# Cross-attention added to 32 batches on one core: four rows per partition and attention by halves of 64 queries

## The reference

```python
q = (tgt @ Wq.T).reshape(B, N, NH, dk).transpose(0, 2, 1, 3)
k = (memory @ Wk.T)...; v = (memory @ Wv.T)...
probs = softmax(einsum('bhqd,bhkd->bhqk', q, k) / sqrt(dk))
att = einsum('bhqk,bhkd->bhqd', probs, v).transpose(0, 2, 1, 3).reshape(B, N, D)
return tgt + att[0]
```

## Time and profile before

| | us |
|---|---|
| median of 3 runs | 190.15 (189.57 to 190.52) |
| profiled execution | 188.74 |
| its span | 186.6 |
| TensorE busy | 127.9 |
| DVE / ACT / POOL busy | 105.7 / 96.3 / 80.7 |

### The profile page before, as it was taken

One profiled execution on the slowest core, in us unless ns is written; L12 is line 12 of the kernel. 1 busy time (PEld: TensorE's weight loads), 2 busy tenths in 40 slices (PEclk: granted clock), 3 DMA queues, 4 the chain that ended last, 5 costly groups with the idle time before them and its releaser, 6 DMA issues.

```text
span 186.6 us, 3382 instructions
## 1 busy us (share of the span) xinstructions
PE 127.9 (69%) x1240; PEld 94.0 (50%) x1240; DVE 105.7 (57%) x171; ACT 96.3 (52%) x225; POOL 80.7 (43%) x45
## 2 busy tenths in 40 slices
PE   6999999999995978998889998798881000000000
PEld 6878877668663756775657666565550000000000
DVE  0455646643709999636699766945618999300000
ACT  2525535566476789679698778898860000000000
POOL 1000000000009999800099996399966999200000
PEclk9999999999999999999999999999999555555555
DMA  6999999999998999999999999999999999999996
GB/s 211 378 359 418 410 409 410 408 407 407 383 410 293 331 332 344 343 305 382 395 386 398 386 367 404 403 407 404 406 416 416 408 422 421 412 418 421 421 421 258
DMA packets 31968, 71.52 MB, mean 383 GB/s; under 512 B 1872, under 2 KB 10064, under 8 KB 31824
## 3 DMA queue, kind: packets, MB, share of 16 engines
q1 hardware_dynamic: 31952, 71.31, 99.9%
HBM read 37.75 MB, written 33.55 MB: 382 GB/s over the span
## 4 chain that ended last, share of the span: by engine, by line
PE 52%; DVE 14%; ACT 13%; issue 6%; DVEq 1%; POOL 0%; ACTq 0%; POOLq 0%
PE bank L387 12%; PE bank L367 8%; ACT probs L586 7%; PE bank L322 6%; PE bank L356 6%; PE bank L345 6%; DVE slots L719 5%; ACT probs_t L594 5%; PE bank L314 5%; PE bank L398 4%; DVE slots L709 3%; DVE neg_max L666 3%; PE bank L469 3%; DVE slots L702 1%; PE bank L409 1%
## 5 line engine op out<-in xcount | busy, mean ns | idle before, releaser
L272 POOL TENSOR_TENSOR slots<-slots,att_rows 128x512 f32<-128x512 f32 (+1 forms) x27 | 43.4, 1650 | 70.0 <-DVE att_rows L691 70.0
L586 ACT ACTIVATE probs<-bank,neg_max 128x512 f32<-128x512 f32 x64 | 44.9, 702 | 12.1 <-DVE neg_max L666 11.7
L666 DVE TENSOR_REDUCE neg_max<-bank 128x1 f32<-128x512 f32 x64 | 41.8, 682 | 11.9 <-PE bank L367 11.8
L387 PE MATMUL bank<-ident,probs 128*128 128x128 f32 x256 | 39.8, 281 | 7.8 <-ACT probs L586 6.7
L594 ACT COPY probs_t<-bank 128x512 f32<-128x512 f32 x64 | 37.7, 592 | 10.8 <-PE bank L387 10.0
L387 PEld LDWEIGHTS bank<-ident,probs 128*128 128x128 f32 x256 | 28.1, 140 | 21.3 <-ACT probs L586 17.1
L367 PE MATMUL bank<-k_t,x_q 32*128 32x512 f32 x192 | 24.1, 425 | 0.0
L278 POOL TENSOR_TENSOR slots<-slots,att_rows 128x1024 f32<-128x1024 f32 x8 | 18.6, 2377 | 4.8 <-DVE att_rows L691 4.8
L286 POOL TENSOR_TENSOR slots<-slots,att_rows 128x2048 f32<-128x2048 f32 x4 | 18.0, 4532 | 3.4 <-DVE att_rows L691 3.4
L702 DVE TENSOR_TENSOR slots<-slots,bank 128x512 f32<-128x512 f32 (+1 forms) x21 | 17.7, 856 | 0.1
L398 PE MATMUL bank<-probs_t,v 128*32 128x128 f32 x512 | 17.3, 276 | 0.7 <-ACT probs_t L594 0.7
(11 more groups left out here) (41 smaller groups left out, 98.6 us busy)
## 6 DMA issues: line engine op xcount, KB each, us to landing
slots<-in_x_dram SPq DMA_DIRECT2D x19, 1024.0 KB, 14.5
slots<-in_x_dram SPq DMA_DIRECT2D x26, 512.0 KB, 8.6
out_dram<-slots SPq DMA_DIRECT2D x13, 1024.0 KB, 14.1
out_dram<-slots SPq DMA_DIRECT2D x22, 512.0 KB, 8.7
out_dram<-slots SPq DMA_DIRECT2D x32, 256.0 KB, 3.6
ctx_raw<-in_ctx_dram SPq DMA_DIRECT2D x1, 1024.0 KB, 4.9
wq_raw<-in_L_xattn_Wq_dram SPq DMA_DIRECT2D x1, 1024.0 KB, 9.1
wv_raw<-in_L_xattn_Wv_dram SPq DMA_DIRECT2D x1, 1024.0 KB, 11.8
```

The source lines that it names most:

```text
L272: nc.gpsimd.tensor_tensor(xs, xs, a.unsqueeze(1).to_broadcast([P, BPS, a.shape[1]]), ALU.add).then_inc(added[g], 1)
L387: last = nc.tensor.transpose(bank[:, PT_BANK + h % 2, t * P:(t + 1) * P], probs[:, h % 2, t * P:(t + 1) * P], ident[:, :])
L586: nc.scalar.activation(probs[:, h % 2, :], bank[:, h % S_BANKS, :], ACT.Exp, bias=neg_max[:, h:h + 1], scale=1.0, accum_out=row_sum[:, h:h ...
L666: nc.vector.tensor_reduce(neg_max[:, h:h + 1], bank[:, h % S_BANKS, :], AX_X, ALU.max, negate=True).then_inc(max_ready, 1)
```

## The change

- A slot holds four adjacent rows per partition of four batches: partition (p, b) holds rows 4p to 4p + 3 of a tile of 128 rows, in 8 KB of memory in one piece. There are 8 groups per row tile and 18 slots. Stores of tiles 0 and 1 are halves of a slot (two rows, 4 KB pieces, 512 KB), those of tiles 2 and 3 whole slots (1 MB).
- Attention goes by halves H of 64 queries (two per tile) with all heads. A unit stacks two heads: partitions 0 to 63 are one head's 64 queries, 64 to 127 another's. Each half has 8 units.
- q and k are kept in fp32 as they are; scores are one full-fp32 matmul per head in a tile of 32 rows and 64 columns, in place of three fp32r passes. k_t needs no low part, and DVE evacuates q_t.
- x of batch 0 is turned by `turn_x0`, 16 matmuls with x as the stationary operand and every fourth column of the identity moving.
- `lay_out_sums` brings row sums to the transposed layout by matmuls, DVE inverts them there, and `normalize` scales the transposed attention while it copies each value four times side by side, for the four batches. `turn_left` and `turn_right` turn it back, the left 256 columns into a PSUM bank for DVE, the right 256 by way of ACT's `copy_right` to SBUF for POOL. DVE adds every left side, POOL every right side; each store waits for both.
- `sum_group` takes the place of `weigh_values`, with 64 moving columns; all four groups of a half share one region of a bank.

The core of the diff follows (within a part, lines that are only removed are mostly left out):

```diff
-BPS = 2
-ROWS = 2
+BATCHES = 4
+ROWS = 4
+HALF = ROWS // 2
...
-    GROUPS = B // BPS
-    SLOTS = GROUPS + 1
-    PAIR = 2
-    PAIRS = HEADS // PAIR
+    GROUPS = B // BATCHES
+    SLOTS = 2 * GROUPS + 2
+    QP = P // ROWS
+    QH = P // 2
+    SIDE = D // 2
+    HALVES = 2 * T
+    UNITS = HEADS // 2
+    PAIRS = UNITS // 2
     S_BANKS = 4
     PT_BANK, BACK_BANK, ATT_T_BANK = 4, 6, 7
-    PT_SLOTS = 6
+    PT_SLOTS = 5
...
+    x_rows = x.rearrange("b (j p r) d -> j p b (r d)", p=QP, r=ROWS)
...
+            def store_half(H, g):
+                sp.wait_ge(left_added, added_through(H, g))
+                sp.wait_ge(right_added, added_through(H, g))
+                sp.dma_start(out_rows[H // 2, :, g * BATCHES:(g + 1) * BATCHES,
+                                      H % 2 * HALF * D:(H % 2 + 1) * HALF * D],
+                             by_batch(slot(H // 2, g, half_rows(H)))).then_inc(stored[H // 2][g], 16)
...
             LAG = 3
             for g in range(GROUPS):
+                store_half(0, g)
             for g in range(GROUPS):
+                store_half(1, g)
                 if g >= LAG:
+                    reload_first(g - LAG)
+            for g in range(GROUPS - LAG, GROUPS):
+                reload_first(g)
             for g in range(GROUPS):
+                store_half(2, g)
+            for g in range(GROUPS):
+                store_half(3, g)
+                if g >= LAG:
+                    reload_second(g - LAG)
+            for g in range(GROUPS - LAG, GROUPS - 2):
+                reload_second(g)
+            for j in range(2, T):
+                for g in range(GROUPS):
+                    store(j, g)
...
+            for H in range(HALVES):
+                out_of_turn_bank(pool, H, RIGHT_SIDE)
+                for g in range(GROUPS):
+                    pool.wait_ge(loaded[H // 2][g], 16)
+                    xs = side_of(H, g, RIGHT)
+                    nc.gpsimd.tensor_tensor(xs, xs, att_right[:, H % 2, :, :], ALU.add).then_inc(right_added, 1)
...
+            def turn_x0(j):
+
+                pe.wait_ge(loaded[j][0], 16)
+                bank_free("x0_t", j)
+                ps = job_bank("x0_t", j)
+                for c in range(C):
+                    for r in range(ROWS):
+                        at = c * P + r * QP
+                        last = mm(ps[:, at:at + QP], slot(j, 0)[:, r, c * P:(c + 1) * P], first_batch,
+                                  start=True, stop=True)
+                last.then_inc(bank_filled, 1)
...
+            def scores(H, m, units):
+
+                queries = slice(H % 2 * QH, (H % 2 + 1) * QH)
+                for s in range(2):
+                    for i in units:
+                        g, rows = 2 * m + s, slice(i * DK, (i + 1) * DK)
+                        last = mm(bank[s * QH:(s + 1) * QH, i, :], q_t[rows, H // 2 % 2, g, queries], k_t[rows, g, :],
+                                  start=True, stop=True, tile_position=(i * DK, s * QH))
...
+            def lay_out_sums(H, m):
+
+                pe.wait_ge(exp_ready, H * UNITS + (m + 1) * HPG)
+                if H > 0:
+                    pe.wait_ge(att_t_ready, sums_through(H, 2 * m) - 1)
+                for s in range(2):
+                    for i in range(HPG):
+                        u = m * HPG + i
+                        last = mm(laid_sums(H, m)[i * DK:(i + 1) * DK, s, :],
+                                  row_sum[:, H % 2, u:u + 1].to_broadcast([P, DK]), ident[:, s * QH:(s + 1) * QH],
+                                  start=True, stop=True, tile_position=(0, i * DK))
+                last.then_inc(sums_laid, 1)
+
+            def sum_group(H, g):
+                m, queries = g // 2, slice(g % 2 * QH, (g % 2 + 1) * QH)
+                out_of_turn_bank(pe, H, m * HPG + HPG - 1)
+                pe.wait_ge(inverse_ready, inverses_through(H, m))
+                if sums_through(H, g) > 1:
+                    pe.wait_ge(att_t_ready, sums_through(H, g) - 1)
                 for t in range(T):
                     for i in range(HPG):
                         h = g * HPG + i
-                        last = mm(att_t_ps[i * DK:(i + 1) * DK, g, :], v[:, t, h * DK:(h + 1) * DK],
-                                  probs_t[:, (j * HEADS + h) % PT_SLOTS, t, :], start=(t == 0), stop=(t == T - 1),
+                        last = mm(bank[i * DK:(i + 1) * DK, ATT_T_BANK, 0:QH], v[:, t, h * DK:(h + 1) * DK],
+                                  probs_t_of(H, m * HPG + i)[:, t, queries], start=(t == 0), stop=(t == T - 1),
                                   tile_position=(0, i * DK))
                 last.then_inc(att_t_summed, 1)
...
+            def turn_rows(ps):
+
+                for r in range(HALF):
+                    for g in range(2):
+                        at = (r * 2 + g) * P
+                        queries = att_t[:, g, r * QP:(r + 1) * QP, :].rearrange("p q b -> p (q b)")
+                        last = nc.tensor.transpose(ps[:, at:at + P], queries, ident[:, :])
+                return last
+
+            def turn_left(H):
+
+                pe.wait_ge(att_t_ready, sums_through(H, 1))
+                if H > 0:
+                    pe.wait_ge(left_added, added_through(H - 1, GROUPS - 1))
+                turn_rows(bank[:, BACK_BANK, :]).then_inc(back_ready, 1)
+
+            def turn_right(H):
+
+                pe.wait_ge(att_t_ready, sums_through(H, HG - 1))
+                turn_bank_free(H, RIGHT_SIDE)
+                turn_rows(turn_bank(H, RIGHT_SIDE)).then_inc(turned, 1)
+
+            def half(H):
+
+                j = H // 2 + 1
+                first, second = H % 2 == 0 and j < T, H % 2 == 1 and j < T
+                turn_probs(H, 0)
+                turn_probs(H, 1)
+                score_pair(H, 2)
+                if first:
+                    pe.wait_ge(att_t_ready, sums_through(H, 0) - 1)
+                    turn_x0(j)
+                if second:
+                    pe.wait_ge(att_t_ready, sums_through(H, 0) - 1)
+                    turn_queries(j)
+                turn_probs(H, 2)
+                turn_probs(H, 3)
+                score_pair(H, 3)
+                if first:
+                    emptied(pe, "x0_t", j)
+                if second:
+                    emptied(pe, "q_t", j)
+                lay_out_sums(H, 0)
+                turn_probs(H, 4)
+                sum_group(H, 0)
+                turn_probs(H, 5)
+                sum_group(H, 1)
+                if H + 1 < HALVES:
+                    score_pair(H + 1, 0)
+                if first:
+                    pe.wait_ge(att_t_ready, sums_through(H, 1))
+                    query_chunk(j, 0)
+                turn_left(H)
+                if first:
+                    query_chunk(j, 1)
+                turn_probs(H, 6)
+                if first:
+                    query_chunk(j, 2)
+                turn_probs(H, 7)
+                if first:
+                    query_chunk(j, 3)
+                    raw_queries_out(j)
+                lay_out_sums(H, 1)
+                if H + 1 < HALVES:
+                    score_pair(H + 1, 1)
+                sum_group(H, 2)
+                sum_group(H, 3)
+                turn_right(H)
...
+            score_four(0, 0)
+            value_chunk(0, 2)
+            value_chunk(0, 3)
             value_chunk(1, 0)
+            turn_probs(0, 0)
             value_chunk(1, 1)
+            turn_probs(0, 1)
             value_chunk(1, 2)
+            turn_probs(0, 2)
             value_chunk(1, 3)
+            turn_probs(0, 3)
+            score_four(0, 1)
             value_chunk(2, 0)
             value_chunk(2, 1)
             value_chunk(2, 2)
             turn_probs(0, 4)
             value_chunk(2, 3)
+            turn_probs(0, 5)
             value_chunk(3, 0)
             value_chunk(3, 1)
+            turn_probs(0, 6)
             value_chunk(3, 2)
+            turn_probs(0, 7)
+            emptied(pe, "v", 2)
+            lay_out_sums(0, 0)
+            lay_out_sums(0, 1)
             value_chunk(3, 3)
+            score_four(1, 0)
+            pe.wait_ge(inverse_ready, inverses_through(0, 1))
+            turn_x0(1)
+            emptied(pe, "v", T - 1)
+            sum_group(0, 0)
+            sum_group(0, 1)
+            turn_probs(1, 0)
+            emptied(pe, "x0_t", 1)
+            turn_left(0)
+            sum_group(0, 2)
+            turn_probs(1, 1)
+            sum_group(0, 3)
+            turn_probs(1, 2)
+            turn_right(0)
+            lay_out_sums(1, 0)
+            score_four(1, 1)
+            turn_probs(1, 3)
+            sum_group(1, 0)
+            sum_group(1, 1)
+            turn_probs(1, 4)
+            turn_left(1)
+            turn_probs(1, 5)
             query_chunk(1, 0)
+            turn_probs(1, 6)
             query_chunk(1, 1)
+            turn_probs(1, 7)
+            lay_out_sums(1, 1)
             query_chunk(1, 2)
+            sum_group(1, 2)
             query_chunk(1, 3)
```

(100 more changed lines are left out.)

659 lines of the change are left out of this document (220 added, 439 removed).

## The result

| | before | after |
|---|---|---|
| median us | 189.86 (188.94 to 190.52, 4 runs) | 247.4 (246.61 to 252.74, 4 runs) |
| profiled execution / span | 188.74 / 186.6 | 247.3 / 245.5 |

The ratio is 1.302, with a 95% interval of 1.294 to 1.310. The forecast was 223 us, its range 203 to 238: the direction was right, and so was the bound (compute in place of DMA); the size was not. Some executions of a kernel, here the one of 252.74, last 1.5% and more above its fastest at a lower mean clock; the ratios leave them out.

A forecast was written before the change was run, and what follows sets the result against it. DMA bounds the kernel before, compute after: 85.0 us to half 2 plus 111.65 for six halves gives 196.7, plus 22.8 a span of 219.5; 2.14 more and times 1.0075 makes 223 us, range 203 to 238.

The forecast's parts named there:

- DMA is no longer the bound; compute sets the pace: Whole kernel: DMA alone would allow a 180.6 us span, but compute arrives too late, giving a span of 219.5.
- holes where they were put: DMA was to stand idle from 59.5 to 66 us, about 77 to 86, and before the last stores.
- A score pair: TensorE, each half: full-fp32 scores of two units, all tiles at once, 1.1 us; four pairs, 4.4.
- the rival that column tiles take turns: TensorE score pairs: column groups over the same rows alternate, 1.95 us a pair, 243 us in all; chance 0.12.
- the 0.5 of the columns: TensorE's sum_group: its time if halving the moving columns halves the earlier 1.01 us.
- the 0.81 of the weight loads: TensorE's sum_group: 32 weight loads alone occupy 0.81 us whatever the columns, so 0.85 was taken.
- the work it lists: TensorE work: 19.9 us in halves 2 and 4, 14.2 in 3 and 5, 13.7 in 6 and 7, against 13.0 before.
- The reciprocal, mis-sized: DVE's reciprocal of laid-out sums, two per half: 0.2 to 0.4 us for 128 columns, 0.2 in the chain.
- The walk: Dependency chain through halves 2 to 7: 23.15, 17.0, 23.15, 17.0, 16.45 and 14.9 us, together 111.65.
- rival D: Whole kernel: TensorE's clock falls from 1.00; waits under 5 us should leave it; no time or chance of its own.
- Prologue and end: Before half 2 and after half 7: turn_probs(2,0) starts at 85.0 us; 22.8 us follow half 7's right side.
- The last stretch: After half 7's right side: a POOL addition 1.28 us, issue and landing 1.6, eight slots 19.9; together 22.8.

The follow-up runs named there:

- run 4: Changed kernel with no attention computed after half 1, whose result is added in halves 2 to 7; all loads, additions and stores stay: 200.5 us.
- run 3: Changed kernel with row sums inverted (128x4) before they are laid out, DVE copying the laid-out inverses instead of 128x128 reciprocals: 231.0 us.
- run 11: Kernel of run 9 plus spare transposes: 14 ahead of turn_probs(2,0), 16 ahead of turning x of tiles 2 and 3: median 212.4 us.
- run 7: Kernel of run 5 with DVE's normalizations 0 and 1 ahead of left adds 6 and 7, and 3 ahead of left add 2: 217.8 us.
- run 1: Changed kernel with 28 spare transposes in the wait ahead of turn_left(1) and 14 ahead of turn_probs(2,0): 248.2 us.
- run 10: Kernel of run 9 with turn_x0's narrow matmuls put back in place of the separate loads of batch 0: 226.41 and 228.95 us.
- run 6: Kernel of run 5 plus some 30 spare transposes per half in TensorE's waits of halves 2 to 7: 224.4 us.
- run 9: Kernel of run 7 with tile 3's load ahead of half 2's stores, half 0's left adds 3 to 5 earlier, turn_left(1) later: median 208.5 us.
- run 5: Kernel of run 3 with batch 0 of x also loaded by itself and turned by four 128-column transposes instead of turn_x0: 220.8 us.

## Why the prediction fell short

Its steps in order, against the trace after (spans: forecast 219.5, measured 245.5).

**DMA is no longer the bound; compute sets the pace:** right. The share is 72.9%, there are holes where they were put (in front of the first stores, before half 1's, before the last), and three that were not (near 45, near 138, and 166 to 190 us), and run 4 shows the pace of transfers alone.

**Prices on TensorE.** A score pair lasts 1.09 us, forecast 1.1; the rival that column tiles take turns is out (two pairs at once, sixteen records, last 1.12). From the start of turn_x0 to that of the next operation it is 3.5 to 3.7 us at full clock, forecast 3.4. lay_out_sums 0.43, forecast 0.45. sum_group is cheaper, 0.65 and 0.59 to the next start (127.19 to 127.78) against 0.85: nearer to the 0.5 of the columns than to the 0.81 of the weight loads. The Trainium skill's 60 cycles per matmul ("TensorEngine Tiling (Array Packing)", Instruction Overhead) would give an estimated 0.8 us if each of the 32 records pays them, and the trace shows less; for the program's 16 matmuls they would give 0.4, so the trace does not decide the rule, only that reading of it. Two of the forecast's sums do not follow from their rows: 32 records in four column groups from 99.20 to 100.21 are 0.126 us each, not 0.106 (with 0.126 a pair comes to 1.01, and 1.02 was measured from start to start), and the work it lists is 6.9, 1.2 and 0.7 us over 13.0 by kind of half, not 2.7 or more in each.

**The reciprocal, mis-sized.** It stood in the chain at 0.2 and in DVE's work at up to 0.4; it measures 0.95, twice per half. The bound was taken from a row of 4 columns (0.17 us), which says next to nothing of 128. Run 3 took 1.5 us and more out of each half with it.

**The walk.** Halves 3 and 5, near full clock, were to take 17.0 each and took 17.9 and 18.0: 1.9 us short, for the reciprocals' 1.5 each are in part made good by the cheap sum_groups. Halves 6 and 7, at 0.87 and 0.88, were to take 16.45 and 14.9 and took 18.4 and 17.9 (half 7 from its first transposes at 203.96 to its copied right side at 221.9), 4.9 us short; run 3, at full clock, brings them to 15.8 and 14.8 by the copies.

**The failed step is rival D**, the clock, dismissed in one sentence: "waits under 5 us in a half of 85% busy should leave it". Halves 2 and 4 were to take 23.15 from one turn_probs(H,0) to the next and took 30.8 (88.5 to 119.3) and 30.5: 15 us of the missing 26, at mean clocks of 0.67. Not all of it is clock: at full clock half 4 takes 20.1 us in run 11, 16 spare transposes included, and with turn_x0 (3.2 us more), the 128-column reciprocals (1.5, run 3) and DVE's old order (0.3, run 7) that makes an estimated 25.1 at most. So up to 2 us of each half's 7.5 are the reciprocals, and 5.5 or more the clock, 11 us for the two.

What the sentence leaned on does not hold: TensorE is busy 77% in half 3 (13.71 of 17.9), which kept its clock, and 86% in half 2, which lost it, and the longest wait of TensorE in these halves is 1.6 us. The runs show two things ahead of a fall. In the kernels without turn_x0 each fall during the attention came where TensorE had been busy 0.8 to 3.8 of the 5 us before it. Such a stretch need not lower the clock: before was busy 3.33 us from 55 to 60 and stayed at 1.00. In the kernels with turn_x0 the clock also fell with TensorE busy for all of the 5 us before, and each such fall came within or right behind a turn_x0 (run 1 at 92.7; runs 3, 4 and 10 in the prologue). That filling waits holds the clock is not shown: run 1 had 1.00 up to turn_x0(2), but run 6 had one low stretch in halves 2 to 7, as run 7 did without spare work, and run 11's mean clock is that of run 9's three shortest executions. In the kernel after, the low stretch of half 2 began at 88.8, ahead of turn_x0(2), behind a wait of 1.6 us, and half 4 had two, from 136.5, ahead of turn_x0(3), and from 143.4, within it. What set off each single fall is not settled, and executions of one kernel differ in it.

**Prologue and end.** turn_probs(2,0) came at 88.5, forecast 85.0, with 13.7 us of the prologue at half clock. The last stretch was 23.6 us, forecast 22.8.

In sum: 3.5 in the prologue, 14.9 in halves 2 and 4, 1.9 in 3 and 5, 4.9 in 6 and 7 and 0.8 at the end make the 26.

**Where the loss comes from, against before.** At full clock and mended, halves 4 and 5 still take 20.1 and 16.2 us (run 11, spare transposes included), 36.3 for a tile that before did in 25.9, and halves 6 and 7 15.3 and 14.7 (run 7). Halves 0 and 1 are ready at 57.6 and 73 (run 9), where DVE normalized the two parts of tile 0 at 55.8 and 66.7; the load of the eighteenth slot, 2.5 us by the forecast's estimate, hides part of that. The best kernels here are 9% over before. No run separated the fp32 scores from the stacking of heads, so what those two alone are worth is open.

## What to carry to other kernels

A kernel whose transfers are the bound may be one whose compute arrives barely in time. Before making transfers leaner, measure the period of the compute that feeds them and set it against the new period of the transfers; the leaner transfers only shorten the time that compute is given. Price a new operation from a row of its own size: a reciprocal of 4 columns tells nothing of one of 128. And when an edit adds waits to TensorE, or replaces wide matmuls by many narrow ones, price a stretch at half clock behind it as a case of its own, with a chance to match.

## What the runs showed of the hardware that was not expected

- The granted clock fell from 1.00 to 0.50 with TensorE never idle, behind the 32 records of turn_x0 (128-column weight loads, 32 moving columns) in run 1, and stayed low to 106 us, although transposes and scores followed. Runs 3, 4 and 10 show it twice each in the prologue; the kernel after had turn_x0(0) without a fall.
- Two kernels with the same prologue had low stretches of different length in it (62.3 to 72.5 us in run 5, 67.8 to 71.2 in run 6), and executions of one kernel differ by 5 to 9 us.
- Some 30 spare transposes of the identity per half cost 1.1 to 1.6 us in halves 5 to 7 (run 6 against run 5, both at full clock).
- A 128x128 reciprocal on DVE from PSUM took 0.95 us, a copy of the same tile 0.29.
- Full-fp32 matmuls in eight tiles of 32x64 at once lasted 1.12 us for 512 columns, four of them 1.09, both at full clock.
- A 256 KB transfer queued at 111 us on a full queue (run 7) could be used at 127.
